# Attention states kept by strips of two heads and read in tiles of 32 rows by 64 columns; the inner gate taken out of PSUM in one copy

## The chip, the cores and the metric

The kernel runs on one core of a Trainium2 chip. The metric is the device time of one execution in microseconds; a shown time is the median over runs. The engines are named as in the profile: PE (TensorE, the matrix engine; PEld is its weight load), DVE (VectorE), ACT (ScalarE), POOL (GpSimd) and SP (SyncE, which here only issues DMAs). PE reads SBUF and writes PSUM, which has eight banks of 128 partitions by 2 KB (512 numbers of f32).

## The reference, cut to what matters

x has 8 rows (batches) of 512 tokens by 512 features. Per row:

```
xn = layernorm(x)
# attention block (16 heads, key width 16, value width 32)
a  = rmsnorm(xn) * ln1
q, k, v, g = a@Wq, a@Wk * scale, a@Wv, a@Wg + bg
gk = log_sigmoid(a @ Wkg1 @ Wkg2 + bkg2) / 16        # Wkg1 is 512 x 16: the "inner gate"
S_t = S_(t-1) * exp(gk_t) + k_t v_t ;  o_t = q_t . S_t   # a scan over tokens, per head
o  = silu(g) * normalized(o) per head
x2 = xn + o @ Wo
s  = x2 + (silu(rmsnorm(x2)@W1) * (rmsnorm(x2)@W3)) @ W2
# gate block: softmax over 8 experts of low rank
out = x + s * silu(sum_e alpha_e * U_e (V_e xn))
```

Products that need full precision are done as three products of high and low parts.

## The kernel before, in words

There are three stages, each over the 8 rows: `phase_f` (layernorm and the gate block), `phase_a` (attention) and `phase_m` (the hidden layer and the output). Each engine has its own instruction stream; semaphores order them. The loops are software pipelined: while the body of a row runs, the parts of the next row are woven in by `ahead(...)`. The body and the parts of `phase_a` are what the change touches.

The scan over tokens is done in NC = 4 chunks c of 128 tokens. Heads and key features lie on partitions: GR = 2 groups g of 8 heads by 16 features, a strip of 32 partitions being two heads. For each chunk PE does, in this order in `body` (L1356 to L1412):

- `weights(i, c)` (L1267, products at L1282): the weights inside the chunk, 64 products per chunk in tiles of 32 rows by 32 columns, into four banks, one for each strip of rows. DVE multiplies them by the causal mask (L1022) into `a_sb`.
- for c < 3: the decayed keys turned (`kt`, L1366); ACT copies them to SBUF (L1203).
- a part of the next row: k0 and k1 at c = 0, u (the inner gate, L1318 and L1320) at c = 1, q0 at c = 2, q1 at c = 3.
- `variance` of the chunk before (L1303), from ACT's squares (L1216).
- for c > 0 the state read (L1390): `state` times the decayed queries, four products of 128 rows by 128 columns ("quads" of four heads) by 128 tokens, into the bank `mix`. The state is kept block-diagonal, 128 by 256 per group, mostly zeros.
- for c < 3 `state_products` (L1351), from which DVE makes the next state: spread over the head mask (L1031) and, for c > 0, decayed and added (L1043).
- the sixteen products of weights and values (L1399), each 32 columns wide, four column strips abreast, into `mix`. ACT squares `mix` (L1216) and copies it (L1219), which frees it.

After the four chunks come, for the next row, z (the key gates, L1329), v0, then the variance of chunk 3, then v1 to v3 and the output gates g0 to g3, and for this row o0 to o3 (all through L160 to L162, 12 products each). ACT's order behind its last copy of `mix` is z (L1140 to L1145), v0, the deviation of chunk 3 (L1231, L1233), `exponentials` (L1156 to L1172), the SiLU of g0 to g3 (L1181). In `exponentials` v1 is copied behind the four exponentials of L1156, v2 and v3 behind those of L1160 and L1162. DVE's `sum_gates` (L945, L950, the scans L954, the three differences L961) feeds them; `gated` (L1063 to L1070) of chunk 3 comes behind, then the weighting of keys and queries (L971 to L994).

PSUM banks are handed out by `Regions`: results take the regions in the order of a list, round robin, and a product waits (`free`) until the result before it in its region has been taken. `dense` has three banks, `mix` one, the weights four. So before, v1's bank was last z1's, g0's was v1's, and g3's was g0's:

```
L845 order = [(None, ["kt0"]), ("k0", ["k0"]), ("k1", ["k1"]), (None, ["ds0", "kt1"]), ("u", ["u"]),
L846          (None, ["var0", "ds1", "kt2"]), ("q0", ["q0"]), (None, ["var1", "ds2"]),
L847          ("q1", ["q1"]), (None, ["var2", "ms"]), ("z", zs), ("v0", values[:1]),
L848          (None, ["var3"]), ("v1", values[1:]), ("g", gates),
```

POOL prepares the attention weights at the start of the span (`prepare_attention_weights`), later it multiplies the loaded xn of the row after by a row factor (`scale`, L1101) and adds squares (L1107). SP issues the loads; the one that POOL's `scale` waits for comes behind a wait for the last `mix` product of a body (L897), a store and a load. In the body of the last row the places of the next row's parts hold first work of `phase_m` (class `Front`).

Of the kernel before, what the change touches and what calls it, by code (L numbers as in the profile page):

```python
# [5 lines left out]
F32 = mybir.dt.float32  # L6
# [50 lines left out]
class Regions:  # L57
# [3 lines left out]
    def __init__(self, counts, name, regions, order, early=()):  # L61
        self.counts, self.name, self.regions = counts, name, regions
        self.where, used = {}, [0] * len(regions)
        for n, result in enumerate(order):
            r = n % len(regions)
            used[r] += 1
            self.where[result] = (r, used[r], 1 if early and result not in early else 0)
# [170 lines left out]
def attention_weights(nc, ctx, KT, D, KD, RANK):  # L238
# [7 lines left out]
    w["wkg1"] = sb("wkg1", [P, KT, 32 + RANK], F32R)  # L246
# [10 lines left out]
def prepare_attention_weights(nc, ctx, pool, w, Wq, Wk, Wkg1, Wkg2, bkg2, Wv, Wg, bg, Wo, ln1_w):  # L257
# [12 lines left out]
    step(pool.memset(w["wkg1"].bitcast(F32), 0.0))  # L270
    RANK, KD = Wkg2.shape
    small = w["stage"][0:RANK, 1, 0:KD]
# [8 lines left out]
    for n, (name, src, kt) in enumerate(jobs):  # L281
# [14 lines left out]
        if name == "wkg1":  # L296
            hi, lo = (w[name][:, kt, at:at + cols] for at in (0, 32))
# [4 lines left out]
    pool.dma_start(small, Wkg2).then_inc(s_small, 16)  # L302
    for dst, src in ((w["bkg2"], bkg2), (w["bg"], bg), (w["ln1"], ln1_w)):
        pool.dma_start(dst, src.rearrange("(m p) -> p m", p=P), allow_slow_non_contiguous=True).then_inc(s_small, 16)
    pool.wait_ge(s_small, 64)
    for at in (0, 32, 96):
        step(pool.tensor_copy(w["wkg2"][at:at + RANK, :], small))
    step(pool.tensor_tensor(w["wkg2"][64:64 + RANK, :], small, w["wkg2"][0:RANK, :].bitcast(F32), ALU.subtract))
# [466 lines left out]
def phase_a(nc, outer, consts, f, shared, w, xn_d, r1_d, xmid_d):  # L775
# [12 lines left out]
    with ctx:  # L788
# [7 lines left out]
        RANK = wkg1.shape[2] - 32  # L796
# [23 lines left out]
        state = [sb(f"state{n}", [P, GR, HG * VH]) for n in range(2)]  # L820
# [7 lines left out]
        psum = [ctx.enter_context(nc.psum_tensor(f"a_ps{b}", [P, 512], F32))[:] for b in range(4)]  # L828
# [3 lines left out]
        for name, per in (("xa_in", 32), ("x2", KT), ("x2sum", KT - 1), ("r2", 1), ("r2_out", 16), ("xn_in", 16), ("xa", KT), ("xahi", KT), ("xalo", KT), ("uhi", 3),  # L832
# [4 lines left out]
                          ("state", GR * (NC - 2)), ("first", NC - 1), ("weighing", NC),  # L837
# [7 lines left out]
        order = [(None, ["kt0"]), ("k0", ["k0"]), ("k1", ["k1"]), (None, ["ds0", "kt1"]), ("u", ["u"]),  # L845
                 (None, ["var0", "ds1", "kt2"]), ("q0", ["q0"]), (None, ["var1", "ds2"]),  # L846
                 ("q1", ["q1"]), (None, ["var2", "ms"]), ("z", zs), ("v0", values[:1]),  # L847
                 (None, ["var3"]), ("v1", values[1:]), ("g", gates),  # L848
                 (None, outs), ("body", [])]
        early = {part: results for part, results in order if part}  # L850
        late = {order[n + 1][0]: results for n, (part, results) in enumerate(order) if not part}
# [1137 lines left out]
```

## Time and profile before

| | |
|---|---|
| median of 3 runs | 1628.15 us (1624.19 to 1628.93) |
| the profiled execution | 1622.4 us, span 1620.7 us |
| PE, PEld | busy 98%, 79% |
| DVE, ACT, POOL | busy 52%, 35%, 10% |
| granted TensorE clock, mean | 0.998 of full |
| attention stage | about 342 to 887 us of the span |
| POOL, busy tenths by slice of 40.5 us, the first nine | 4 7 7 0 0 0 0 1 0 |

The busy shares say which engine sets the pace; the order of time says where one engine waits for another. A matmul of f32 stands as two records in the trace, so "x8" at L1390 are four products; the record's duration includes the modelled tail, and the distance from one start to the next is what it costs.

### The profile page before, as it was taken

The numbers are of one execution on the slowest core, as the hardware profiler recorded it, in microseconds if no ns is written. First come the engines' busy times: TensorE is split into PE (matmuls) and PEld (weight loads), VectorE is DVE, ScalarE is ACT, GpSimd is POOL, SyncE is SP. The second block draws the span as 40 slices with busy tenths as digits, with TensorE's granted clock in tenths as the row PEclk, the third lists the DMA queues.
The fourth block names the chain that finished last, engine by engine and source line by source line (L and its number), as shares of the span: only waits on it lengthen the run. The fifth ranks groups of instructions, "written<-read, shape, count | busy, mean of one in ns | idle before, by whom it ended". The sixth has DMA issues, their size and how long they took to land.

```text
span 1620.7 us, 30581 instructions
## 1 busy us (share of the span) xinstructions
PE 1593.2 (98%) x12274; PEld 1277.6 (79%) x12274; DVE 847.3 (52%) x1311; ACT 567.2 (35%) x982; POOL 167.2 (10%) x190
## 2 busy tenths in 40 slices
PE   7999999999999999999999999999999999999998
PEld 5777888777777777777777788888888888888886
DVE  5565455367797887978876451331415142241413
ACT  4333343366564645636564411111111111111111
POOL 4770000100220102101020000000000000000000
PEclk9999999999999999999999999999999999999999
DMA  7563332101020210202213423030301203030200
GB/s 175 151 135 78 83 95 69 59 27 52 9 84 0 84 53 32 84 0 84 84 54 118 144 101 127 0 136 0 136 0 49 87 0 136 0 136 0 91 14 26
DMA packets 50700, 113.16 MB, mean 70 GB/s; under 512 B 13321, under 2 KB 24665, under 8 KB 42466
## 3 DMA queue, kind: packets, MB, share of 16 engines
q1 hardware_dynamic: 47906, 99.95, 19.5%
q10 hardware_dynamic: 1152, 8.39, 1.3%
q0 software_dynamic: 1600, 4.25, 0.9%
q8 instruction: 28, 0.46, 0.1%
q14 instruction: 14, 0.11, 0.0%
HBM read 78.98 MB, written 33.59 MB: 69 GB/s over the span
## 4 chain that ended last, share of the span: by engine, by line
PE 94%; DVE 2%; ACT 1%; issue 1%; DMA 1%; PEld 0%; SPq 0%; ACTq 0%; DVEq 0%; PEldq 0%
PE m_ps L1529 10%; PE m_ps L1531 10%; PE m_ps L1530 10%; PE a_ps L160 7%; PE a_ps L162 7%; PE a_ps L161 7%; PE f_ps L160 5%; PE f_ps L162 5%; PE f_ps L161 5%; PE m_ps L1543 5%; PE m_ps L1544 5%; PE m_ps L1545 5%; PE a_att L1282 3%; PE a_ps L1399 2%; PE a_ps L1303 2%; PE a_ps L1390 1%
## 5 line engine op out<-in xcount | busy, mean ns | idle before, releaser
L1529 PE MATMUL m_ps<-m_xshi,m_w 128*128 128x512 f32 x680 | 268.1, 394 | 1.4 <-DVE m_w L1520 1.4
L1766 DVE TENSOR_TENSOR m_h<-m_ps,m_silu 128x512 f32<-128x512 f32 x85 | 58.7, 690 | 402.4 <-PE m_ps L1531 402.4
L1531 PE MATMUL m_ps<-m_xshi,m_w 128*128 128x512 f32 x680 | 266.5, 392 | 0.0
L1530 PE MATMUL m_ps<-m_xslo,m_w 128*128 128x512 f32 x680 | 266.4, 392 | 0.0
L1830 ACT ACTIVATE m_silu<-m_ps 128x512 f32<-128x512 f32 x85 | 50.8, 597 | 334.3 <-PE m_ps L1531 334.3
L1529 PEld LDWEIGHTS m_ps<-m_xshi,m_w 128*128 128x128 f32 x680 | 127.7, 188 | 30.0 <-issue 2.1
L1531 PEld LDWEIGHTS m_ps<-m_xshi,m_w 128*128 128x128 f32 x680 | 127.6, 188 | 28.7
L1530 PEld LDWEIGHTS m_ps<-m_xslo,m_w 128*128 128x128 f32 x680 | 127.7, 188 | 28.1 <-issue 0.2
L1101 POOL TENSOR_TENSOR row<-row,a_r 128x512 f32<-128x512 f32 x32 | 50.7, 1615 | 331.6 <-DMA a_r<-scratch_r 331.6
L1022 DVE TENSOR_TENSOR a_a<-a_att,causal 128x1024 f32<-128x1024 f32 x64 | 75.2, 1216 | 11.8 <-PE a_att L1282 11.8
L1839 ACT ACTIVATE m_h0hi<-m_h 128x512 fp32r<-128x512 f32 x46 | 29.1, 632 | 135.7 <-DVE m_h L1766 135.7
L1543 PE MATMUL m_ps<-m_h0hi,m_w 128*128 128x512 f32 x192 | 75.3, 392 | 0.0
L1544 PE MATMUL m_ps<-m_h0lo,m_w 128*128 128x512 f32 x192 | 75.3, 392 | 0.0
L1545 PE MATMUL m_ps<-m_h0hi,m_w 128*128 128x512 f32 x192 | 75.3, 392 | 0.0
L1839 ACT ACTIVATE m_h1hi<-m_h 128x512 fp32r<-128x512 f32 x39 | 24.7, 632 | 115.6 <-DVE m_h L1766 115.6
L1107 POOL TENSOR_TENSOR a_cum<-a_cum 128x512 f32<-128x512 f32 x24 | 30.7, 1281 | 321.3 <-ACT a_cum L1190 321.3
L1543 PE MATMUL m_ps<-m_h1hi,m_w 128*128 128x512 f32 x160 | 62.6, 391 | 0.0
L1544 PE MATMUL m_ps<-m_h1lo,m_w 128*128 128x512 f32 x160 | 62.6, 391 | 0.0
L1545 PE MATMUL m_ps<-m_h1hi,m_w 128*128 128x512 f32 x160 | 62.6, 391 | 0.0
L160 PE MATMUL f_ps<-f_xnhi,f_w1hi 128*128 128x512 f32 x128 | 52.1, 407 | 2.5 <-DVE f_xnlo L476 1.2
L160 PE MATMUL a_ps<-a_wvhi,a_xahi 128*128 128x512 f32 x128 | 53.1, 415 | 0.0
L160 PE MATMUL a_ps<-a_xahi,a_wghi 128*128 128x512 f32 x128 | 50.8, 397 | 0.9 <-ACT a_v_tok L1149 0.6
(306 smaller groups left out, 3487.9 us busy)
## 6 DMA issues: line engine op xcount, KB each, us to landing
row<-scratch_xn SPq DMA_DIRECT2D x16, 1024.0 KB, 4.9
row<-scratch_xmid SPq DMA_DIRECT2D x16, 1024.0 KB, 7.3
m_xt<-in_L_attn_W SPq DMA_DIRECT2D x33, 256.0 KB, 3.2
f_xt<-in_L_attn_x SPq DMA_DIRECT2D x32, 256.0 KB, 8.1
scratch_xn<-row SPq DMA_DIRECT2D x8, 1024.0 KB, 9.0
scratch_gate<-row ACTq DMA_DIRECT2D x8, 1024.0 KB, 3.9
scratch_xmid<-row SPq DMA_DIRECT2D x8, 1024.0 KB, 3.9
row<-scratch_gate SPq DMA_DIRECT2D x8, 1024.0 KB, 10.5
```

Source lines behind the costliest of these rows:

```text
L160: pe.matmul(out, lh, rh, start=first and n == 0, stop=False)
L161: pe.matmul(out, lh, rl, start=False, stop=False)
L162: ins = pe.matmul(out, ll, rh, start=False, stop=last and n == end)
L1022: dve.tensor_tensor(a_sb[n].rearrange("p s g o t -> p (s g o) t"), ps, bcast(causal, 1, 4 * GR), ALU.mult).then_inc(att.taken_sem(f"{c}_{n ...
L1529: pe.matmul(ps, wh, xh, start=k == 0, stop=False)
L1530: pe.matmul(ps, wh, xl, start=False, stop=False)
L1531: ins = pe.matmul(ps, wl, xh, start=False, stop=k == LAST)
L1543: pe.matmul(ps, lh, rh, start=j == 0, stop=False)
L1544: pe.matmul(ps, lh, rl, start=False, stop=False)
L1545: ins = pe.matmul(ps, ll, rh, start=False, stop=j == FT - 1)
L1766: dve.tensor_tensor(h[n], dense.region(f"b{j}"), silu[n], ALU.mult).then_inc(dense.taken_sem(f"b{j}"), 1)
L1839: act.activation(h_hl[n][0], h[n], ACT.Copy).then_inc(count.sem("hhi"), 1)
```

## The change

The state is kept as 128 by 64 per group: a strip of 32 partitions holds its own two heads. The state read takes each strip of 32 rows with its 64 columns, eight products per chunk in place of four. The output of a chunk lies in halves of two banks, EVEN and ODD, for even and odd quads. The turned keys get the other half of ODD. `dense` has two banks of its own and, outside the chunks, ODD as a third; which result takes which is written out in `places`. PE turns the keys of chunks 1 and 2 behind the next row's part, and waits for ACT's copy of them before the state read. z moves behind v0 and the last variance on PE, and behind them and the deviation on ACT. The weights of the inner gate are laid out in four copies (three high, one low) so that one copy on ACT takes all 64 rows out and DVE subtracts one part. POOL prepares these weights.

```diff
@@ attention_weights, prepare_attention_weights
-    w["wkg1"] = sb("wkg1", [P, KT, 32 + RANK], F32R)
+    w["wkg1"] = sb("wkg1", [P, KT, 4 * RANK], F32R)
...
+            copies = [w[name][:, kt, n * RANK:(n + 1) * RANK] for n in range(4)]
+            for copy in copies[1:3]:
+                step(pool.tensor_copy(copy, s))
+            hi, lo = copies[0], copies[3]
@@ phase_a, banks
-        psum = [ctx.enter_context(nc.psum_tensor(f"a_ps{b}", [P, 512], F32))[:] for b in range(4)]
+        psum = [ctx.enter_context(nc.psum_tensor(f"a_ps{b}", [P, 512], F32))[:] for b in range(2)]
+        ps_mix = ctx.enter_context(nc.psum_tensor("a_mix", [P, 2, 512], F32))[:]
...
+        order = [("k0", ["k0"]), ("k1", ["k1"]), (None, ["ds0"]), ("u", ["u"]), (None, ["var0", "ds1"]),
+                 ("q0", ["q0"]), (None, ["var1", "ds2"]), ("q1", ["q1"]), (None, ["var2", "ms"]),
+                 ("v0", values[:1]), (None, ["var3"]), ("z", zs), ("v1", values[1:]), ("g", gates),
+                 (None, outs), ("body", [])]
+        places = {result: n for n, results in enumerate((
+            ["k0", "ds0", "var0", "q0", "ds2", "var2", "v0", "z1", "v3", "g2", "o1"],
+            ["k1", "u", "ds1", "var1", "q1", "ms", "var3", "v1", "g0", "g3", "o2"],
+            ["z0", "v2", "g1", "o0", "o3"])) for result in results}
...
+        dense = Regions(count, "dense", psum + [ps_mix[:, ODD]], ..., places)
+        turned = Regions(count, "kt", [ps_mix[:, ODD, GR * P:]], list(range(NC - 1)))
+        mix = Regions(count, "mix", [ps_mix[:, :, 0:QD // 2 * P]], list(range(NC)))
@@ vector: inner_gate
-                dve.tensor_copy(u[0:RANK], ps).then_inc(count.sem("uhi"), 1)
-                dve.tensor_copy(u[64:64 + RANK], ps).then_inc(count.sem("uhi"), 1)
-                dve.tensor_copy(u[96:96 + RANK], at.region("u")[32:32 + RANK]).then_inc(count.sem("uhi"), 1)
                 dve.wait_ge(*count.at("uhi", i))
-                dve.tensor_tensor(u[32:32 + RANK], ps, u[0:RANK].bitcast(F32), ALU.subtract)...
+                dve.tensor_tensor(u[low], at.region("u")[low], u[low].bitcast(F32), ALU.subtract)...
@@ vector: the next state
-                        for g in range(GR):
-                            ins = dve.tensor_tensor(new[:, g, :]..., bcast(ds[:, g], 1, HG // 2), bcast(hmask...), ALU.mult)
+                        dve.tensor_tensor(new.rearrange("p g (o v) -> p g o v", v=VH), ds,
+                                          bcast(bcast(parity, 1, GR), 3, VH), ALU.mult)...
@@ scalar
+            def inner_gate(i, at=dense):
+                act.wait_ge(*at.ready("u", i))
+                act.activation(u[0:4 * RANK], at.region("u")[0:4 * RANK], ACT.Copy).then_inc(count.sem("uhi"), 1)
...
-                    for part in (("k0", "k1"), ("c1",), ("q0",), ("q1",))[c]:
+                    for part in (("k0", "k1"), ("u",), ("q0",), ("q1",))[c]:
                         ahead(part)
+                    if 0 < c < NC - 1:
+                        keys(i, c)
...
-                ahead("z")
                 ahead("v0")
                 inverse_deviation(i, NC - 1)
+                ahead("z")
                 ahead("exponentials")
@@ tensor: body
+                    for part in (("k0", "k1"), ("u",), ("q0",), ("q1",))[c]:
+                        ahead(part)
+                    if 0 < c < NC - 1:
+                        pe.wait_ge(*mix.taken(c - 1, i))
+                        turned_keys(i, c)
                     if c > 0:
                         variance(i, c - 1)
...
+                    if 0 < c < NC - 1:
+                        pe.wait_ge(*turned.taken(c, i))
...
-                        for quad in range(QD):
-                            g, first_head = quad * HQ // HG, quad * HQ % HG
-                            pe.matmul(ps[:, quad, :], state[c % 2][:, g, first_head * VH:(first_head + HQ) * VH],
-                                      qhat[:, gcs[g], :], start=quad == 0, stop=True, skip_group_check=True)
+                        for g in range(GR):
+                            for strip in range(4):
+                                rows, at = slice(H32 * strip, H32 * (strip + 1)), H64 * (strip % 2)
+                                pe.matmul(ps[2 * g + strip // 2][at:at + H64], state[c % 2][rows, g, :],
+                                          qhat[rows, gcs[g], :], start=g == 0, stop=True, skip_group_check=True,
+                                          tile_position=(H32 * strip, at))
...
-                ahead("z")
                 ahead("v0")
                 variance(i, NC - 1)
+                pe.wait_ge(*mix.taken(NC - 1, i))
+                ahead("z")
                 ahead("v1")
                 ahead("g")
```

The `Front` class takes v0 in place of v1 for one of its products, in the same order of work.

## Rows read from the trace of the kernel before

**Rows 1.** The page: busy time, share of the span and instructions of each engine.
```profile
PE 1593.2 (98%) x12274; PEld 1277.6 (79%) x12274; DVE 847.3 (52%) x1311; ACT 567.2 (35%) x982; POOL 167.2 (10%) x190
```

**Rows 2.** Busy time by stretch: stretch, length, busy us of each engine, clock.
```profile
434.60:501.05 66.45, 66.45 (x939) 52.30 (x943) 53.73 (x72) 37.17 (x66) 10.05 (x7) 1.00 0.13 51
```

**Rows 3.** PE's waits over the span: total us, times, longest.
```profile
PE a_ps L160 <- ACT a_v_tok L1149: 0.6, 2, 0.5
...
PE a_ps L160 <- ACT row L1181: 0.3, 1, 0.3
```

**Rows 4.** PE in order of time, z to g3: start, length, line, records.
```profile
466.39 0.73 PE L1329 MATMUL a_ps<-a_u,a_wkg 128*128 128x512 f32 x2
466.95 0.39 PE L160 MATMUL a_ps<-a_wvhi,a_xahi 128*128 128x512 f32 x1
...
478.81 0.39 PE L160 MATMUL a_ps<-a_xahi,a_wghi 128*128 128x512 f32 x1
...
487.20 0.40 PE L160 MATMUL a_ps<-a_xahi,a_wghi 128*128 128x512 f32 x1
```

**Rows 5.** ACT in order of time, |z| to the first SiLU; idle before in brackets.
```profile
467.50 1.27 ACT L1140 ACTIVATE a_soft<-a_ps,a_bkg 128x512 f32<-128x512 f32 x2
...
475.52 2.29 ACT L1156 ACTIVATE a_lv<-a_lv 128x512 f32<-128x512 f32 x4 [2.67 <-DVE a_lv L961]
477.72 0.58 ACT L1149 ACTIVATE a_v_tok<-a_ps 128x512 f32<-128x512 f32 x1
...
480.24 1.06 ACT L1149 ACTIVATE a_v_tok<-a_ps 128x512 f32<-128x512 f32 x2
...
486.26 1.84 ACT L1181 ACTIVATE row<-a_ps,a_bg 128x512 f32<-128x512 f32 x3
```

**Rows 6.** PE in order of time around chunk 1 and chunk 2.
```profile
447.19 1.02 PE L1303 MATMUL a_ps<-a_sq,avg 128*128 128x512 f32 x2
448.05 1.05 PE L1390 MATMUL a_ps<-a_neg,a_state 128*128 128x128 f32 x8
449.03 0.43 PE L1351 MATMUL a_ps<-a_v_tok,a_fold 128*32 128x64 f32 x16
449.28 1.06 PE L1399 MATMUL a_ps<-a_a,a_v_tok 128*32 128x128 f32 x32
450.27 0.34 PE L1282 MATMUL a_att<-a_qx,a_lv 32*32 32x128 f32 x12
...
451.89 0.44 PE L1366 MATMUL a_ps<-ident,a_soft 128*128 128x128 f32 x2
452.08 0.48 PE L160 MATMUL a_ps<-a_xahi,a_wqhi 128*128 128x512 f32 x1
```

**Rows 7.** DVE in order of time: the first of three inner gate casts.
```profile
447.42 0.67 DVE L931 CAST a_u<-a_ps 16x512 fp32r<-16x512 f32 x1
```

**Rows 8.** ACT in order of time: the deviation of chunk 0, the copy of mix.
```profile
448.25 0.69 ACT L1231 ACTIVATE a_rn<-a_ps,eps 128x512 f32<-128x512 f32 x1 [1.80 <-PE a_ps L1303]
...
452.85 0.60 ACT L1219 ACTIVATE a_oc<-a_ps 128x512 f32<-128x512 f32 x1 [1.85 <-DVE a_rn L1063]
```

**Rows 9.** POOL in order of time: its scaling in the first two looped rows.
```profile
406.82 7.87 POOL L1101 TENSOR_TENSOR row<-row,a_r 128x512 f32<-128x512 f32 x4 [17.28 <-DMA a_r<-scratch_r]
...
478.88 6.21 POOL L1101 TENSOR_TENSOR row<-row,a_r 128x512 f32<-128x512 f32 x4 [21.25 <-DMA a_r<-scratch_r]
```

**Rows 10.** DVE in order of time: the differences L961 in both rows.
```profile
406.14 3.47 DVE L961 TENSOR_TENSOR a_lv<-a_cum 128x1024 f32<-128x1024 f32 x2
409.53 2.31 DVE L961 TENSOR_TENSOR a_dq<-a_cum 128x1024 f32<-128x1024 f32 x1
...
474.26 2.36 DVE L961 TENSOR_TENSOR a_lv<-a_cum 128x1024 f32<-128x1024 f32 x2
```

**Rows 11.** Busy time by stretch at the span's end; PE first, the clock after POOL.
```profile
1610.10:1613.00 2.90, 0.00 (x0) 0.00 (x0) 2.79 (x6) 0.00 (x0) 0.00 (x0) 1.00 0.00 0
...
1614.00:1616.00 2.00, 1.95 (x10) 1.55 (x8) 0.58 (x1) 0.00 (x0) 0.00 (x0) 0.50 0.00 0
```

More of the change, by code:

```diff
@@ L57, with __init__ @@
 class Regions:
-    def __init__(self, counts, name, regions, order, early=()):
+    def __init__(self, counts, name, regions, order, early=(), places=None):
         self.counts, self.name, self.regions = counts, name, regions
@@ L269, in prepare_attention_weights @@
     step(pool.memset(w["wkg2"].bitcast(F32), 0.0))
[L270 removed]
     RANK, KD = Wkg2.shape
[L272 removed]
+    small = w["stage"][0:4 * RANK, 1, 0:KD]
     sources = {"wkg1": Wkg1, "wk": Wk, "wq": Wq, "wv": Wv, "wg": Wg, "wo": Wo}
@@ L819, in phase_a @@
         kt_sb = flat(w["fold"]).rearrange("p (g t) -> p g t", g=GR)
-        state = [sb(f"state{n}", [P, GR, HG * VH]) for n in range(2)]
+        state = [sb(f"state{n}", [P, GR, 2 * VH]) for n in range(2)]
         sq, oc, rn = sb("sq", [P, QD, P]), sb("oc", [P, QD, P]), sb("rn", [P, QD, P])
@@ L1196, in deviation, with keys, by_quads @@
                 act.activation(added[0:1], added[0:1], ACT.Exp, scale=-0.5).then_inc(count.sem("r2"), 1)
+            def keys(i, c):
+                act.wait_ge(*turned.ready(c, i))
+                act.activation(flat(kt_sb), turned.region(c), ACT.Copy).then_inc(turned.taken_sem(c), 1)
+            def by_quads(ap):
+                return ap.rearrange("p (g b) t -> p g b t", b=2)
             def body(i, ahead):
@@ L1354, in state_products, with turned_keys @@
                 ins.then_inc(dense.ready_sem(f"ds{c}"), 1)
+            def turned_keys(i, c):
+                pe.wait_ge(*turned.free(c, i))
+                ps = turned.region(c)
+                for g in range(GR):
+                    ins = pe.transpose(ps[:, g * P:(g + 1) * P], khat[:, g * NC + c, :], ident)
+                ins.then_inc(turned.ready_sem(c), 1)
             def body(i, ahead):
@@ L1379, in body @@
                     pe.wait_ge(*mix.free(c, i))
-                    ps = mix.region(c).rearrange("p (q t) -> p q t", t=P)
+                    ps = [mix.region(c)[:, (EVEN, ODD)[quad % 2], quad // 2 * P:(quad // 2 + 1) * P] for quad in range(QD)]
+                    if 0 < c < NC - 1:
+                        pe.wait_ge(*turned.taken(c, i))
                     if c > 0:
@@ L1433, in tensor @@
             f.tensor(pe, first_row)
-            for part in ("v0", "v1", "g"):
+            parts["v0"](0)
+            pass_over(pe, dense, ["z1"], 0)
+            for m in range(KT):
+                pe.wait_ge(*f.dense.taken(f"u{m}", NB - 1))
+            for part in ("v1", "g"):
                 parts[part](0)
```

107 lines of the change are left out of this document (46 added, 61 removed).

## The prediction

> **What bounds the kernel now.** I read the page's busy times first, then the engines by stage, then PE's waits, then the order of time around the changed places. PE is busy for 98% of the span [rows 1] and for every one of the 66.45 us of an attention row in the middle of that stage [rows 2]; in that row DVE has 53.7 us of work and ACT 37.2. So work taken off PE there comes off the time, work taken off DVE or ACT buys nothing by itself, and any new wait of PE is paid whole. PE's waits in the attention stage are few, and they point at the tight place: for ACT's copy of values (L1149) and for ACT's SiLU of the output gate (L1181), 0.9 us in all [rows 3]. Both are waits of output-gate products (g0, g1 and g3) for a PSUM bank. So I followed the chain that frees these banks: gate products z on PE, absolute value, exponential and logarithm on ACT (L1140 to L1145), sums on DVE (L945 to L961), exponentials on ACT (L1156), and only then ACT's copy of v1 (L1149), behind it v2, v3 and, 8.5 us after the copy of v1, the first SiLU.
>
> In the row of 434.6 to 501.05 PE starts z0 at 466.39 and v0 at 466.95 [rows 4]. ACT starts |z| at 467.50, copies v1 in 477.72 to 478.30, v2 at 480.24, and SiLUs g0 in 486.26 to 486.95 [rows 5]. PE starts g0 at 478.81 and g3 at 487.20 [rows 4]. So the chain has 0.51 us to spare at g0 and 0.25 us at g3.
>
> **The change, part by part.**
> *State read (c = 1 to 3).* Now four products of 128 rows by 128 columns: L1390 starts at 448.05 and L1351 at 449.03, 0.98 us [rows 6]. After: eight products in tiles of 32 rows by 64 columns. L1399 runs sixteen products of 128 moving columns in four column strips in 0.99 us up to the next line's start [rows 6], so a set of four abreast takes at most 0.25 us. If four row strips run abreast too, two sets take 0.50 us, and I add 0.12 us for a second change of tile shape (L1399's four sets of 0.22, as one of L1390's four, leave about that before the 32x32 tiles): 0.62, a gain of 0.36. Bounds: two abreast 0.98 + 0.1, a loss of 0.1; none abreast eight times 0.22 + 0.1 = 1.9, a loss of 0.9. Gains beyond 0.5 would need more than four abreast, which four strips exclude. I take the four, since the 64 products of L1282, which lie in four row strips, take 1.62 us (450.27 to 451.89 [rows 6]), 0.025 each, which no stream of one after the other gives.
>
> The Trainium skill (TensorEngine Tiling, Restrictions and Gotchas) says that different row tiles cannot access the same PSUM bank at once. Strips 0 and 1 share a bank here, 2 and 3 the other, so by that rule it would be two abreast and the loss of 0.1; in this trace L1282 gives every row strip a bank of its own, so no row decides it. It is a rival below.
>
> *Keys turned later (c = 1, 2).* The transposes (0.19 us, 451.89 to 452.08 [rows 6]) move behind u or q0 and behind the mix bank's release, and PE must wait for the keys' copy before the state read. Let U be the end of u (447.19). Transposes and variance (0.86) bring PE to U + 1.05. ACT begins the new u copy at U + 0.23 (DVE's cast did [rows 7]) and the keys' copy 0.5 later; at half the columns of a copy of 0.60 [rows 8] I give it 0.4: U + 1.13, so PE waits 0.1. The mix bank is free earlier: its copy for c = 1 ends at 453.45 [rows 8], and PE wants it behind q0, twelve products of 0.23 from 452.08, at 454.9. The bank of ds1 needs DVE's one subtraction: U + 0.23 + 0.60 + 0.04 + 0.68 = U + 1.55, and PE comes at U + 1.15 + 0.62. Queued on ACT behind the u copy are keys and the deviation, none late. So per body 0.36 + 2 x 0.26 = 0.88 gained, over eight bodies 7.0 us.
>
> *Inner gate in one copy.* Matmul count and moving columns stay (64 and 48 weight columns for 48 and 16), PE nothing. DVE loses three casts (2.1 us a row [rows 7]) and most of the state arithmetic. Both lie beside PE: nothing; at worst DVE's later start would be hidden by the same spare. The longer weight preparation on POOL (eight small copies, three DMAs) is part of its work in the span's first three of forty slices, in the table above; the attention stage comes in the ninth: nothing.
>
> *z behind v0 and the last variance, on PE and ACT.* This is the part that costs. z0 now lies in the bank of the mix, so z goes behind v0 and var3 (0.86 [rows 6]). Between 466.95 and 478.81 lie var3 and 48 value products, 0.229 each; v0 is twelve of them, 2.75 us [rows 4]. In the same row, with v0 at 466.39: var3 at 469.14, z0 at 470.00. ACT is moved too: its logarithm of var3 starts 1.06 after that product (447.19 to 448.25 [rows 6, 8]), so 470.20, lasts 0.69, its exponential 0.63, and |z0| starts at 471.44 in place of 467.50: 3.94 late. v1's bank is now var3's, read till 470.89: PE waits 0.35 there. The chain has no other slack: ACT idles 2.67 us ahead of L1156 for DVE [rows 5], and DVE runs without a gap from the first logarithm's end. DVE's L961 so starts at 474.26 + 3.94 = 478.20.
>
> Here a second thing joins. POOL's scaling of the next x (L1101) starts at 478.88 [rows 9], released by loads that hang on the last mix product, which does not move. In the first looped row it started at 406.82, and there L961's first two and its third took 3.47 and 2.31 us where the undisturbed pair took 2.36 [rows 9, 10]: 2.3 us each beside POOL for 1.17 alone. After the change every row is like that: first L961 to 479.84, second to 482.1, third to 484.4. ACT: exponentials (1.15 the pair) to 483.35, v1 copied 483.25 to 483.85, so g0 starts at 483.90 where PE is ready at 479.2, a wait of 4.7. Then L1160 at 484.45 (waits for the third), v2 at 486.51, 6.27 later than before, and SiLU of g0 from 492.53 to 493.2. g1 waits 0.45 more (v2's bank), g3 0.5 more (g0's). g3 starts 6.27 - 0.25 = 6.0 us late, and so all behind it. Without POOL it would be 3.94 - 0.25 = 3.7.
>
> That is late next and nothing gives it back: the outputs o0 to o3 find DVE free (its weighting ends about 498, o0 at 499), the next body's waits move along. Seven rows are prepared this way (the eighth body has only the next stage's work in these places). The first of them already had POOL and 0.92 us of waits [rows 3]; its L961 would start about 410.8 and its SiLU come about 5 late. Sum: 6 x 6.0 + 5 = 41 lost, 7.0 gained, 34 slower. On the profiled execution's 1622.4 us (span 1620.7) that is 1656.4; the median of the runs lies 5.75 above it, so 1662.
>
> **Rivals.**
> 1. *Two strips abreast* (the shared bank): 24 reads lose 0.1 in place of gaining 0.36, and two a body wait 0.1, so 3 lost for 7 gained: 1672. For: no row shows two row strips in one bank. Against: the column strips of L1399 do share one and run abreast. 20%.
> 2. *POOL does not slow DVE, or starts elsewhere*: 7 x 3.7 - 7 = 19 slower, 1647. For: POOL's start is a DMA's end. Against: [rows 9, 10]. 12%.
> 3. *The clock falls.* After PE's only long gap late in the span (nothing in 1610.1 to 1613.0) the granted clock is 0.50, 1.2 GHz, in 1614 to 1616 [rows 11]. A wait of 4.7 us in every row could do that. g0 at half rate is 2.8 longer; g1 and g3 wait 0.95 anyway, so 1.85 at most is exposed, 13 us over seven rows: up to 1675. Some of it is likely; as a case of its own (over 6 us) 15%.
> The Trainium skill (TensorE: Matmul & The Clock Gate, What's actually happening) says that an idle engine is throttled to 1.2 GHz and activity releases it; [rows 11] agree as to the fall.
> 4. *Faster.* One mechanism: the late z is absorbed before g0, so that only the state read counts: 7 gained, 1621. It decides if the chain from |z| to the copy of v1 has over 3.9 us of slack. For it: DVE is 3 to 4 us a row lighter. Against: that work lies ahead of the chain, and the spare is 0.51 and 0.25 [rows 4, 5]. 7%. That the strips do not run abreast at all: 24 x (0.9 + 0.36) more, 1692, 2%.
>
> **How the numbers follow.** My forecast (four abreast, POOL beside DVE, no more than 6 us from the clock) has 41%: 1662, own range 1656 to 1670. With rivals 1 to 3 on either side the range is 1644 to 1678, leaving out the faster case and the serial strips. A change of 0.3% (4.9 us) is what a measurement can tell. Slower 0.90: all but rival 4 and what lies between; same 0.03, where several of my terms fail at once; faster 0.07.
>
> **What would show it.** In the trace after: PE idle about 4.7 us ahead of the first g product, released by L1149's counterpart, and shorter ones ahead of g1, g3 and v1; |z| about 5 us behind z's old place in the row; L961 near 2.3 us in every row; a PE distance of 0.6 from the state read to the state product; a row of 66.4 + 6.0 - 0.9 = 71.5 us. Wrong if g0 has no wait, if the rows are shorter than 66.4, or if the time from the start of the state read to the next line is near 1.1.

## The result and the profile after

| | before | after |
|---|---|---|
| median | 1628.32 us (1624.19 to 1628.93, 4 runs) | 1676.76 us (1674.34 to 1679.72, 4 runs) |
| ratio | | 1.0314, 95% interval 1.0297 to 1.0332 |
| span of the profiled execution; of a second one | 1620.7; 1622.4 | 1676.9; 1673.6 |

The change makes the kernel 3.1% slower. 1662 (1644 to 1678) was forecast: the direction was right, 15 us of the loss were missing between the medians (20 between the profiled executions, which the parts below are taken from), and by its ratio, 1.0314, the result lies just outside the range, whose upper end is 1.0306 of the 1628.15 it was worked out from.

Words used below: a *body* is one pass over a row's four chunks. There are eight, in three groups: the first pass of the loop (the *first body*), its six later passes (the *looped rows*), and the *last body*, which is written out behind the loop. A wait *marked issue* is time in which PE was idle and waited for nothing that the profile shows. A *narrow* read has tiles of 32 by 64, a *wide* one of 128 by 128.

The page after: busy time, then the chain that ended last. PE's share fell from 98% to 96% of a longer span [rows 1]; DVE's part of the chain is 5% (2% before).
```profile
PE 1608.0 (96%) x12466; PEld 1272.8 (76%) x12466; DVE 821.6 (49%) x1263; ACT 575.0 (34%) x990; POOL 178.1 (11%) x199
...
PE 88%; DVE 5%; issue 3%; ACT 2%; DMA 1%; PEld 0%; SPq 0%; DVEq 0%; ACTq 0%; PEldq 0%
```
PE's waits after (total us, times, longest). The first line answers to L1149's 0.6 us in [rows 3]: it is the wait of g0 in all seven prepared rows.
```profile
PE a_ps L161 <- ACT a_v_tok L1158: 30.4, 7, 7.0
...
PE a_att L1303 <- issue: 6.1, 5, 2.0
...
PE a_ps L161 <- ACT a_rn L1252: 2.2, 7, 0.3
PE m_ps L1566 <- DVE m_w L1557: 2.2, 1, 2.2
...
PE a_ps L161 <- DVE a_xalo L938: 1.5, 1, 1.5
PE a_ps L161 <- PEq L146: 1.2, 1, 1.2
```
Where the time went, by stretch: stretch, length, busy us of PE, PEld, DVE, ACT, POOL, granted clock. First before, cut at its starts of the value products of the first row, the first body, the second, the last, and the place behind its last o product:
```profile
342.33:364.62 22.29, 22.29 (x97) 17.80 (x95) 11.78 (x15) 15.21 (x27) 0.00 (x0) 1.00 0.12 49
364.62:434.62 70.00, 67.47 (x932) 52.04 (x931) 53.41 (x71) 41.73 (x72) 11.71 (x7) 1.00 0.09 35
434.62:501.00 66.38, 66.38 (x932) 52.25 (x931) 53.73 (x72) 37.17 (x66) 10.05 (x7) 1.00 0.13 51
501.00:833.00 332.00, 332.00 (x4652) 261.25 (x4651) 268.66 (x360) 188.25 (x333) 50.28 (x35) 1.00 0.14 55
833.00:885.10 52.10, 50.72 (x862) 39.84 (x861) 39.75 (x60) 26.67 (x46) 3.86 (x3) 1.00 0.25 83
```
Then after, cut at the same places:
```profile
343.46:367.21 23.75, 22.56 (x97) 17.72 (x95) 11.87 (x15) 15.21 (x27) 0.00 (x0) 1.00 0.11 46
367.21:450.51 83.30, 71.53 (x955) 53.70 (x955) 49.51 (x65) 42.38 (x73) 9.35 (x7) 0.92 0.08 30
450.51:522.25 71.74, 67.52 (x955) 51.25 (x955) 49.95 (x66) 38.21 (x67) 11.87 (x7) 0.98 0.12 48
522.25:882.34 360.09, 338.98 (x4772) 257.18 (x4771) 249.82 (x330) 193.42 (x338) 58.80 (x35) 0.97 0.13 50
882.34:936.76 54.42, 50.60 (x885) 37.99 (x885) 37.92 (x57) 27.00 (x46) 3.86 (x3) 1.00 0.24 80
```
Each kernel has a second profile (e12 of after, e13 of before). The loss is the difference of the means over the two, 53.7 us between the spans; between the medians it is 48.4:

| part | before | after | loss | forecast |
|---|---|---|---|---|
| up to the first value products | 342.3, 343.2 | 343.5, 342.1 | 0 | 0 |
| values and gates of the first row | 22.3, 22.3 | 23.75, 23.7 | 1.4 | 0 |
| first body (the loop's first pass) | 70.0, 70.0 | 83.3, 80.7 | 12.0 | 4.1 |
| six bodies | 398.4, 398.4 | 431.8, 431.4 | 33.2 | 30.7 |
| last body and all behind it | 787.7, 788.6 | 794.6, 795.6 | 7.0 | -0.9 |

Five of the six looped rows of after take 71.7 us in the first profile and the last takes 73.25, because the granted clock is 0.50 for longer in it (856.6 to 863.4).

The first looped row of after (450.51 to 522.25) in order of time (start, length; idle before in brackets), PE first, as in [rows 4, 6]. The state read takes 0.59 us from its start to the next line, 0.98 before; |z| waits for z0 and z0 for v0 and the variance:
```profile
479.85 0.67 PE L1420 MATMUL a_mix<-a_neg,a_state 32*64 32x128 f32 x16
480.44 1.08 PE L1430 MATMUL a_mix<-a_a,a_v_tok 128*32 128x128 f32 x32
481.45 0.51 PE L161 MATMUL a_ps<-a_wvhi,a_xahi 128*128 128x512 f32 x1
...
484.33 1.02 PE L1324 MATMUL a_ps<-a_sq,avg 128*128 128x512 f32 x2
484.79 0.79 PE L1350 MATMUL a_mix<-a_u,a_wkg 128*128 128x512 f32 x1
...
486.13 0.50 PE L161 MATMUL a_ps<-a_wvhi,a_xahi 128*128 128x512 f32 x1 [0.32 <-ACT a_rn L1252]
...
498.55 0.79 PE L161 MATMUL a_ps<-a_xahi,a_wghi 128*128 128x512 f32 x1 [3.90 <-ACT a_v_tok L1158]
```
ACT in that row, as [rows 5]: |z0| 5.20 us behind the next products' start (481.45), 1.11 before; then the idle for L972, the copy of v1, the first SiLU.
```profile
486.65 0.67 ACT L1149 ACTIVATE a_soft<-a_mix,a_bkg 128x512 f32<-128x512 f32 x1
...
494.66 1.15 ACT L1165 ACTIVATE a_lv<-a_lv 128x512 f32<-128x512 f32 x2 [4.39 <-DVE a_lv L972]
...
497.92 0.58 ACT L1158 ACTIVATE a_v_tok<-a_ps 128x512 f32<-128x512 f32 x1
...
507.15 0.69 ACT L1190 ACTIVATE row<-a_ps,a_bg 128x512 f32<-128x512 f32 x1
```
DVE's differences L972 in it and, in the first body, its scans L965 (before: four scans 1.37 us), both beside POOL's scaling:
```profile
415.13 4.53 DVE L965 TENSOR_TENSOR_SCAN a_cum<-ones,a_neg 128x128 f32<-128x128 f32 x4
419.59 1.69 DVE L961 TENSOR_TENSOR a_neg<-a_neg,a_soft 128x512 f32<-128x512 f32 x1
...
493.40 3.43 DVE L972 TENSOR_TENSOR a_lv<-a_cum 128x1024 f32<-128x1024 f32 x2
496.75 2.29 DVE L972 TENSOR_TENSOR a_dq<-a_cum 128x1024 f32<-128x1024 f32 x1
```
POOL's scaling in the two bodies:
```profile
415.22 5.51 POOL L1106 TENSOR_TENSOR row<-row,a_r 128x512 f32<-128x512 f32 x4 [20.49 <-DMA a_r<-scratch_r]
...
493.85 8.03 POOL L1106 TENSOR_TENSOR row<-row,a_r 128x512 f32<-128x512 f32 x4 [20.50 <-DMA a_r<-scratch_r]
```
The Trainium skill (SBUF — State Buffer, SBUF: two separate sides) says that DVE instructions with two SBUF inputs and GpSimd instructions that read SBUF shut each other out of a shared port for whole instructions. The trace agrees: a difference of L972 doubles from 1.2 to 2.3 us, and takes 1.23 again where POOL's work is cut (e4).

### The profile page after: what moved, and what is told of

Same layout as the page of the kernel before. It is cut to its first block, busy times and chain, and to the rows that moved or that the text cites. A ratio compares the mean times of both kernels' runs of the same rounds, so it can differ in the third digit from the quotient of the medians.

```text
span 1676.9 us, 30976 instructions
## 1 busy us (share of the span) xinstructions
PE 1608.0 (96%) x12466; PEld 1272.8 (76%) x12466; DVE 821.6 (49%) x1263; ACT 575.0 (34%) x990; POOL 178.1 (11%) x199
## 3 DMA queue, kind: packets, MB, share of 16 engines
q10 hardware_dynamic: 1152, 8.39, 1.2%
## 4 chain that ended last, share of the span: by engine, by line
PE 88%; DVE 5%; issue 3%; ACT 2%; DMA 1%; PEld 0%; SPq 0%; DVEq 0%; ACTq 0%; PEldq 0%
PE m_ps L1566 9%; PE m_ps L1568 9%; PE m_ps L1567 9%; PE f_ps L161 5%; PE a_ps L161 5%; PE f_ps L163 5%; PE f_ps L162 5%; PE m_ps L1580 5%; PE m_ps L1582 5%; PE m_ps L1581 5%; PE a_ps L163 5%; PE a_ps L162 5%; PE a_att L1303 3%; PE a_mix L1430 2%; PE a_ps L1324 2%
## 5 line engine op out<-in xcount | busy, mean ns | idle before, releaser
L1106 POOL TENSOR_TENSOR row<-row,a_r 128x512 f32<-128x512 f32 x32 | 58.6, 1859 | 322.9 <-DMA a_r<-scratch_r 322.9
L161 PE MATMUL a_ps<-a_xahi,a_wghi 128*128 128x512 f32 x96 | 43.4, 452 | 30.4 <-ACT a_v_tok L1158 30.4
L1303 PE MATMUL a_att<-a_qxd,a_dk 32*32 32x64 f32 x2048 | 49.5, 225 | 3.3 <-issue 3.3
```

The costliest lines, as they stand in the source:

```text
L161: pe.matmul(out, lh, rh, start=first and n == 0, stop=False)
L1303: return pe.matmul(ps[s:s + H32, strip % 2, g, :, at:at + q.shape[2]], keys[rows, g * NC + c, s:s + H32], q[rows], start=True, stop=True, ...
```

## The experiments

The ratios are to the runs of before that were made with each experiment, and so do not follow from the medians shown.

**The parts one by one: e1, e2, e3, e8.** e1 is before with z moved only; e2 is after with z first again; e3 is after with the wide read; e8 is before with the new inner gate.
```diff
# e1, in before, PE (the same on ACT); regions as in after
-                ahead("z")
                 ahead("v0")
                 variance(i, NC - 1)
+                ahead("z")
# e2, in after: z0, z1, v0 in regions 0, 1, ODD
+                ahead("z")
+                pe.wait_ge(*mix.taken(NC - 1, i))
                 ahead("v0")
                 variance(i, NC - 1)
-                pe.wait_ge(*mix.taken(NC - 1, i))
-                ahead("z")
# e3, in after
-  pe.matmul(ps[2 * g + strip // 2][at:at + H64], state[c % 2][rows, g, :], qhat[rows, gcs[g], :], ...)  # 8 a read
+  pe.matmul(ps[quad], state[c % 2][:, g, first_head * VH:...], qhat[:, gcs[g], :], ...)                 # 4 a read
```


> The kernel before with one edit: z behind v0 and the variance of chunk 3, on PE and on ACT, with the regions that the change gives them; the state read, the banks of mix and the inner gate stay as before. Theory (the place of z is what costs): the whole loss and none of the gain, so per looped row the measured +5.3 us of the change and the 0.9 us that its state read gives back, 6.2 us; with the first row and the last body as they were measured (+13 and +8), 1628 + 6 x 6.2 + 13 + 8 = 1686 us, and g0 waits about 4 us for the v1 copy in each looped row. Rival (the cost sits in the shared bank of mix and the inner gate's new copy on ACT): near 1628 us, and g0 waits as before. Second rival (instruction fetch or the clock, and not the late z, made the first row and the last body dear): rows +6.2 but the rest as before, 1665 us.

> The changed kernel with z put back ahead of v0 on PE and ACT: z0 and z1 take regions 0 and 1, and v0 takes the bank that mix shares, so v0 waits for ACT's last copy of mix instead of z. Theory: the loss of the change goes and its gain of 7.0 us (0.36 per state read, less the key wait) stays; v0 waits about 0.7 us per row (ACT is done 1.11 us after the products' end in the rows of before, the two z products cover about 0.45), 7 rows, 5 us: 1628.3 - 7.0 + 5 = 1626 us, between 1621 and 1631. Rival (the late z is not the cause, the loss lies in the two banks or in ACT's copy of the inner gate): over 1650 us. If the first row and the last body keep their part of the loss, +10 to +20 on 1626.

> The changed kernel with the state kept block-diagonal again and read in four products of 128 by 128 instead of eight of 32 by 64; z, banks and inner gate as changed. Theory (the narrow read gives 0.36 us a read, 21 to 24 reads, and lies on the path): 1676.8 + 0.36 x 21 = 1684 us, and a read takes 0.95 us where the change shows 0.59. Rival (the gain of the read is swallowed by the wait of g0, since both end at the same copy): within 2 us of 1677. Second rival (the extra products cost instruction time elsewhere): below 1675, and the waits marked issue go.

> The kernel before with the inner gate's part of the change alone (64 rows of products, one copy by ACT, one difference by DVE, the weights laid out for it). Theory (it costs nothing: it lies beside the products of q and the variance): within 1 us of before, a ratio of 0.999 to 1.001. Rival (the 4 us by which the quads read of the changed kernel is dearer than the late z alone come from it, by way of ACT's order or POOL's preparation of the weights): +3 to +4 us, a ratio of 1.002.

| | median | ratio | looped row |
|---|---|---|---|
| e1 late z only | 1676.1 | 1.0319 (1.0301 to 1.0336) | 71.6 to 73.9 |
| e2 z first | 1633.9 | 1.0057 (1.0040 to 1.0074) | 66.4 to 66.5 |
| e3 wide read | 1681.0 | 1.0344 (1.0324 to 1.0364) | 72.9 to 74.0 |
| e8 inner gate only | 1626.75 | 1.0011 (0.9999 to 1.0024) | 66.3 |

The place of z alone makes as large a loss as the whole change (e1: 1.0319 for 1.0314), and taking it back gives all but 0.6% back (e2). e1's first rival, a cost in the shared bank or in the inner gate's copy, falls. Its second, that something else made both ends of the loop dear, falls for the first body and holds for the last, as the stretches show; that is why e1 came out 10 us under what was expected. The three other parts together come to nothing in the span, but not in each stretch. e1 takes 79.8 us in its first body (9.8 over before), 437.2 in the six looped rows (38.8 over) and 788.0 from the last body on (as before). So the other parts win 5.6 us in the looped rows of the change, and lose about 2 in its first body and all of its 7.0 from the last body on. e3 is 5 us above the change (ratios 0.0030 apart). Its looped row has 1.35 us more of reads (1.09, 1.06 and 0.98 from start to next start, for 0.60, 0.59 and 0.59), 9 us over the rows, but its waits marked issue are 2.4 us less (1.7 against the second profile of after) and its end 3.2 us shorter (both below): the narrow read is on the path, and about half of what it wins is lost outside the looped rows. e2's v0 waits as expected:
```profile
PE a_mix L161 <- ACT a_oc L1240: 4.3, 7, 0.6
```

**POOL beside DVE: e4.**
```diff
-  pool.tensor_tensor(xa[:, m, :], xa[:, m, :], by, ALU.mult)
+  pool.tensor_tensor(xa[:, m, 0:16], xa[:, m, 0:16], by[:, 0:16], ALU.mult)
```
This kernel leaves out the row factor for 496 of the 512 tokens.

> The changed kernel with POOL's scale of xn cut to 16 of 512 tokens per instruction (most of the row factor is left out of the computation). Theory (DVE's differences and scans are stretched while POOL works beside them, 3.43 us against 2.3, and 4.53 against 1.37 in the first row): each looped row's g0 wait falls from 3.9 to about 1.6 us, the first row's by 3 or more: 6 x 2.3 + 3.5 = 17 us less, 1659 us. With no wait long enough for a fall of the clock, 1.65 us per row more: 1648 us. Rival (DVE's stretch comes from ACT or from PE reading beside it, not from POOL): L972 stays at 3.4 us and the time within 2 us of 1677.

1662.3 us, 1.0228 (1.0205 to 1.0251). L972's pair is back to 2.38 us, and g0 waits for
```profile
PE a_ps L161 <- ACT a_v_tok L1158: 19.8, 7, 2.8
```
that is 2.8 in every row: POOL costs 1.1 us of this wait in a looped row (not the 2.3 expected, since only the pair ahead of the v1 copy counts, and it starts undisturbed) and 4.2 in the first body, where the scans take 1.37 us again. The looped rows are of two kinds, and the granted clock tells them apart; three of the six are like the first line, three like the second:
```profile
443.91:513.43 69.52, 66.35 (x955) 50.10 (x954) 45.81 (x66) 38.02 (x67) 7.67 (x7) 1.00 0.13 49
513.43:584.28 70.85, 67.70 (x955) 51.41 (x954) 45.80 (x66) 38.13 (x67) 7.67 (x7) 0.98 0.12 48
```
So behind a wait of 2.8 us the clock falls in some rows and not in others, and here a fall costs 1.3 us of the row.

**The clock: e5, e11.** Both put products that nobody reads into PE's wait ahead of g0, so that PE stays busy: 32 of 256 columns (e5), 14 of 512 (e11).
```diff
 def output_gates(i):
+    for _ in range(32):   # e11: 14, into a bank of the weights, 512 columns
+        pe.matmul(ps_mix[:, EVEN, 256:512], wg[0][:, 0, 0:P], xa_hl[0][:, 0, 0:256], start=True, stop=True, ...)
```


> The changed kernel with 32 products of 128 by 128 by 256 ahead of g0, into a half bank that nobody reads, some 3.4 us of work in a wait of 3.9 us. Theory (each looped row loses about 1.5 us to the granted clock of .50 behind the wait for the v1 copy): the wait stays but the first products of g0 come 0.24 us apart instead of 0.43; g takes 11.2 us a row instead of 12.7, 6 x 1.5 = 9 us, and with the first row's fall 10 to 12 us less: 1666 us. Rival (the fall follows from the row's whole share of work and only moves elsewhere, or the products cost what they save): within 2 us of 1677. If they last longer than the wait, each row is later by the difference.

> As e5 with 14 products of 128 by 128 by 512 in place of 32 short ones, about 3.2 us of work in the wait ahead of g0, into a bank of the weights, not in the prologue. Theory (the fall of the clock behind that wait costs 1.5 us a looped row, and e5 lost it again to instruction waits in every row, 2.7 us, because of its many short products): g takes 11.2 us behind the filling, few waits marked issue in the loop, rows of 70.2 us, 1667 us. Rival (any PE instructions added to the loop bring its instruction waits): rows of 73 and more, 1690 us.

In after the clock behind the wait of g0 is at the lower level, 1.2 GHz (one stretch of each row):
```profile
498.20:501.60 3.40, 3.05 (x7) 2.47 (x8) 3.37 (x3) 2.79 (x4) 3.40 (x2) 0.50 0.00 0
```
In e11 it stays at 2.4 GHz through the whole row,
```profile
449.10:520.54 71.44, 70.02 (x969) 52.83 (x968) 50.03 (x66) 38.12 (x67) 11.81 (x7) 1.00 0.12 48
```
and two other waits come out that the slow products had covered:
```profile
493.16 3.43 PE L1362 MATMUL a_att<-a_xahi,a_wghi 128*128 128x512 f32 x14
497.25 0.50 PE L161 MATMUL a_ps<-a_xahi,a_wghi 128*128 128x512 f32 x1 [0.67 <-ACT a_v_tok L1158]
...
500.49 0.50 PE L161 MATMUL a_mix<-a_xahi,a_wghi 128*128 128x512 f32 x1 [0.17 <-ACT a_v_tok L1158]
...
506.63 0.50 PE L161 MATMUL a_ps<-a_xahi,a_wghi 128*128 128x512 f32 x1 [0.28 <-ACT row L1190]
```
g1 starts 3.24 us behind g0 (2.80 at full speed in [rows 4] spacing, twelve of 0.234), g3 9.38 behind it (8.39 there). The row is 71.4 us for 71.7: the fall of the clock costs 1.5 us where it happens and only 0.3 to 0.5 of the row (71.9 in the second profile), because g1's and g3's banks would be late anyway. In e4, where they are not, it cost 1.3. e11: 1671.9 us, 1.0293 (1.0264 to 1.0321), a smaller gain than the 1667 expected. e5 fails in another way: 1700.0 us, 1.0462 (1.0441 to 1.0482). In its first looped row the g0 products run at full speed too, but the loop's code no longer stays loaded; its filling of the first row's wait, before the loop, costs another 3.7 us (27.4 for 23.75). The instruction transfers (queue, packets, MB) in six rows of e5,
```profile
q8 instruction: 54, 0.88, 0.8%
```
and in the same six of e11, as of after and before:
```profile
q8 instruction: 1, 0.02, 0.0%
```
With 987 PE records to a row (e5) nine transfers come in every pass, and PE has waits marked issue in each, 17.5 us over the six; with 969 (e11) it has none. In e5's first looped row they are 2.7 us:
```profile
PE a_ps L1339 <- issue: 1.4, 1, 1.4
PE a_att L1303 <- issue: 1.3, 1, 1.3
```

**A free bank for z: e6.** z1 goes into a bank of the weights, which is free between the last mask and the next row's weights; v0 takes region 1.
```diff
 # in e2
-  dense = Regions(count, "dense", psum + [ps_mix[:, ODD]], ...)
+  dense = Regions(count, "dense", psum + [ps_mix[:, ODD], ps_att[1][:, 1]...], ...)   # fourth: z1
```


> As e2 (z first, narrow read, two banks, new inner gate), but no product waits for ACT's last copy of mix: z1 goes into one of the banks of the weights, whose chunk 3 is masked by then, v0 into region 1, and only the variance of chunk 3 and v3 use the shared bank. Theory: z takes 0.56 us of a row instead of 1.35, 7 x 0.8 = 5.6 us, and the first v0 no longer waits for the stage before, 3 us: 1633.9 - 8.6 = 1625 us, level with before (1624.6) within 0.3%: a row of 65.6 to 65.8 us against 66.39, so 4 to 5 us won in the rows, and given back by the waits marked issue in the first row and the last body, 5 us more than before. Rival (those waits are not the narrow read's and go with another layout): 1620 us, a ratio of 0.997. Rival (the wait moves to the variance of chunk 3 or to v1): over 1630.

1627.2 us, 1.0007 (0.9996 to 1.0018). The looped row is won, as expected:
```profile
436.98:502.59 65.61, 65.61 (x955) 50.37 (x955) 49.72 (x66) 37.76 (x67) 10.02 (x7) 1.00 0.13 52
```
It is 0.8 us a row under before's 66.4, 4.8 over six; the first body is 1.7 longer and the part from the last body on 2.6 to 3.4. So the narrow read is worth 0.8 us a row where nothing waits, 5 us in the looped rows, and these are given back outside them.

**What gives it back: e9, e10, e14, e15, e16.** PE's waits marked issue are 1.4 us in both profiles of before, 6.6 and 5.9 in those of after. e9 is before with each read product cut in two by tokens; e10 is e6 with the wide read in the last body; e14 is before with the keys turned behind the next row's part; e15 is e6 with the keys ahead of it, in banks of their own; e16 is e15 with the old inner gate.
```diff
# e9, in before
+    for t in (slice(0, H64), slice(H64, P)):
-        pe.matmul(ps[:, quad, :], state..., qhat[:, gcs[g], :], start=quad == 0, ...)
+        pe.matmul(ps[:, quad, t], state..., qhat[:, gcs[g], t], start=quad == 0 and t.start == 0, ...)
# e14, in before, PE and ACT, c = 1, 2
-    keys()
     ahead(part)
+    keys()
```


> The kernel before with each of the four products of a state read cut in two by tokens, so that PE has as many instructions per read as in the changed kernel (8 and not 4), and everything else as it was. Theory (it is the number of PE instructions in the unrolled first row and last body that brings the waits marked issue, 6.6 us in the changed kernel against 1.4): those waits rise to 4 to 7 us, beside what the read itself takes more (0.98 now, perhaps 1.2: 21 x 0.2 = 4 us); 1632 us together. Rival (they come with the change's tiles or with where the code lies, not with the count): under 3 us, the looped rows longer only by the reads.

> As e6, but the unrolled first and last rows keep the block-diagonal state and read it in four products of 128 by 128, while the six looped rows read it in eight of 32 by 64. Theory (the narrow products, which follow each other faster, are what makes PE wait for its instructions in the unrolled rows): the waits marked issue fall from e6's 5.8 us to the 1.4 to 4.2 of the kernels with quads there, the reads of the two rows give back 6 x 0.39 = 2.3 us, the looped rows stay at 65.6: 1624.5 to 1627 us, a ratio of 0.998 to 1.001. Rival (the waits are those of the layout with two banks): still 5 us or more, and 1629 us.

> The kernel before with one edit: in chunks 1 and 2 the keys are turned behind the next row's part (u, q0) and not ahead of it, on PE and on ACT, as the change has it; wide read, one bank, old inner gate. Theory (it is this order that brings the waits marked issue: every kernel with it had 4.2 to 6.6 us of them in the first row and the last body, every kernel without it 1.4 to 2.8): 4 us or more of such waits, the looped rows at 66.4 to 66.6, ratio 1.002 to 1.003. Rival (they come from the two banks or the narrow read, or from where the code happens to lie): 1.4 to 2.8 us, ratio 1.000 to 1.001.

> Narrow read, two banks, z first with z1 in a bank of the weights and the new inner gate, as e6, but the keys turned ahead of the next row's part, in banks of their own as before. Theory (order of the keys): rows of 65.5 us, waits marked issue back to 1.4 to 2.8 us, 1622 us where before is 1625.5, ratio 0.998. Rival (the waits stay): 65.5 a row and 5 us of them, ratio 1.000 to 1.001. The reads may start 0.1 to 0.2 us earlier, since the shared bank no longer holds the keys.

> As e15 with the inner gate of before. Theory (the inner gate's part gives 0.1 us a looped row or nothing, as e8 showed): within 0.1% of e15, ratio 0.998 to 0.999. Rival (its copy on ACT and the longer preparation by POOL cost 1 to 2 us before the first row): 1.5 us faster than e15.

| | median | ratio | looped row | issue, first body / last body |
|---|---|---|---|---|
| before, twice | | | 66.4 | 0 / 1.4 |
| e8 | | | 66.3 | 1.2 / 0.6 |
| e1 | | | 71.6 to 73.9 | 1.4 / 0.8 |
| e9 | 1649.1 | 1.0143 (1.0128 to 1.0158) | 68.8 | 1.3 / 1.5 |
| e14 | 1638.6 | 1.0085 (1.0067 to 1.0102) | 67.75 | 1.6 / 2.1 |
| e3 (two banks, wide read) | | | 72.9 to 74.0 | 1.3 / 2.9 |
| e10 | 1629.45 | 1.0027 (1.0016 to 1.0037) | 65.6 | 1.6 / 3.8 |
| e16 | 1636.6 | 1.0067 (1.0054 to 1.0080) | 67.1 | 1.4 / 3.3 |
| e6 | 1627.2 | 1.0007 | 65.6 | 2.0 / 3.2 |
| e15 | 1625.7 | 1.0011 (0.9996 to 1.0026) | 65.6 | 1.7 / 4.2 |
| e2 | | | 66.4 to 66.5 | 1.3 / 4.9 |
| after, twice | | | 71.7, 71.9 | 2.9, 2.2 / 3.7, 3.7 |

In the attention stage of these kernels such waits lie in the loop's first pass and the last body only, where code runs for the first time. (The first body, too, belongs to the loop and is not unrolled, against what I wrote ahead of e9 and e10.) None of my theories explains them alone: not the count of instructions (e9: 2.8 us in the two bodies), not the narrow products (e10, whose last body has none and waits 3.8 us), not the order of the keys (e14 has 3.7, between what the theory and its rival wanted; e15, with the old order, has 5.9). Kernels with `mix` in two banks have 4.2 us or more in the two bodies (e3 the least) and the others 3.7 or less (e14 the most). The two profiles of after differ by 0.7, more than lies between e3 and e14, so this is no clean line either; the cause is open. e9's 17 us above what was expected are mostly its reads, 1.82 us each for 0.98, 2.5 a row (last section).

e14 and e16 brought something else. Their looped rows lose 1.3 and 1.5 us to one wait that neither before nor after has (PE's waits in e14):
```profile
PE a_ps L1355 <- DVE a_u L935: 8.9, 7, 1.3
```
The old inner gate, three casts and a difference on DVE, still holds u's bank when the state product of chunk 1 wants it; with the new one the wait is gone (e15 against e16: 10.9 us between the medians, 1.5 us a row). I had put the new inner gate at nothing, which is true of before's banks (e8) and false of the change's.

**The same code again: e12, e13.**

> The changed kernel, unaltered, for a second profile of the same code. The theory of steps (first row, six rows, last body) wants the same looped rows of 71.7 us and the same 7 us wait in the first row; if the 3.7 us at the very end (11.3 us from the last transposes to the end of the span, against 7.6) is chance, it comes out at 7 to 9 us here, and the waits marked issue show how much they move by themselves.

> The kernel before, unaltered, for a second profile. If the start of the attention stage (342.3 us in the first profile, 343 to 344 in the kernels whose stage before is the same) moves by 1 us, and the waits marked issue (1.4 us) move too, then 1 to 2 us of the difference between two profiles belong to no edit; the looped rows must come out at 66.4.

Of e12 by stretch, first body and second:
```profile
365.86:446.56 80.70, 69.58 (x955) 52.30 (x954) 49.51 (x65) 42.38 (x73) 9.35 (x7) 0.94 0.08 31
446.56:518.46 71.90, 67.70 (x956) 51.47 (x955) 49.95 (x66) 38.22 (x67) 11.76 (x7) 0.98 0.12 47
```
Rows repeat within 0.2 us. The first body does not: 2.6 us less here, with k and q1 at full speed, where the first profile had them at the lower clock, 1.5 us more each; the second has it for longer around g0's wait instead. The end is no chance: from the last transposes to the end of the span it takes 11.3 and 10.9 us, 7.6 and 8.4 in before. After, SP's issues of the four output stores:
```profile
1669.43 4.74 SPq L1766 DMA_DIRECT2D out<-m_xt  x4
```
Before:
```profile
1616.14 2.12 SPq L1729 DMA_DIRECT2D out<-m_xt  x4
```
In the last 12 us of after, two instruction transfers fall between the first store and the end, none in before's:
```profile
q14 instruction: 2, 0.02, 0.5%
```
The other traces bear out that these transfers go with the late stores. Of the seventeen profiles, five (after, e12, e4, e5, e11) have two transfers 5.5 to 5.8 and 3.3 to 3.6 us before the end; in each the second store comes 3.3 us behind the first, and the end takes 10.1 to 11.3 us. The twelve others have none in the last 10 us; there the stores are 0.6 us apart and the end takes 7.0 to 8.4, in e3 too (8.1), which is after with the wide read. No run moved the transfers and nothing else, so that they delay the stores is likely and not shown.

## Why the prediction was off

The step that failed is the carrying over of the looped row's sum to the bodies at both ends of the loop: they were priced at 4.1 and -0.9 us and cost 12.0 and 7.0. The items follow the prediction's terms.

- *What bounds the kernel, and the step that costs*: right. z behind v0 is the loss, by the chain |z|, DVE, exponentials, v1, g0. e1 and e2 show it. In the looped rows e3, e6, e8 and e15 clear the other parts.
- *State read*: 0.59 us for 0.62 forecast, so four strips run abreast (two would need 1.08), though strips 0 and 1 share a bank. Rival 1 is refuted. The rule of the Trainium skill (TensorEngine Tiling (Array Packing), Restrictions and Gotchas) that different row tiles cannot access one PSUM bank at the same time does not hold here, for two row strips that write different partitions of it. Strips that write the same partitions of a bank were not tried. The gain in a looped row is 0.76 (1.17 from the reads, less 0.2 ahead of the reads of chunks 1 and 2 together, and 0.2 ahead of chunk 3's), not 0.88.
- *The looped row*: 71.5 forecast, 71.7 and 71.9 measured. That this is so near is in part luck, since terms cancel (forecasts in brackets). v1 waits 0.32 (0.35). g0 waits 3.9 (4.7): POOL's start falls 0.45 us behind the start of the first difference and stretches the pair by 1.05 (1.5, from 478.20 to 482.1 for 2.36), and PE comes to g0 0.4 later. That is because z1's region is v0's, which was not counted: z1 waits for v0's copy, which ends at 485.13, and z takes 0.4 more. g1 and g3 do not wait (0.95), since g0 at the lower clock is 1.5 longer; e11 takes the fall of the clock away and finds them at 0.44 and 0.55, as forecast.
- *The first body*: this term failed, 12.0 against 4.1. I took "POOL was there already" for "little more to lose", with L961 moved and POOL fixed. But the chain moved so that POOL met the scans, 4.53 us for 1.37, and g0 waits 7.0 us; e4 takes 4.2 of it away. e1, where only z is late, has the same 7.0 us wait and 9.8 of the 12.0. To these come waits marked issue of 2.9 and 2.2 us (none before, 1.4 in e1) and, in one profile of two, 3.1 of the clock. The 410.8 that the prediction gives for L961's start here should by its own 3.94 be 410.1, which changes little.
- *The last body and the end*: this term failed, 7.0 against -0.9. The prediction said only that this body prepares no row, and counted nothing for it but the read's gain; no row I used showed the waits marked issue, and I took unrolled code as free. 2.3 us are these, 3.1 lie behind the last transposes (2.6 of them SP's later stores), and 0.8 and 0.6 are a longer wait for `m_w` (2.2 and 2.05 us for 1.4 and 1.5). In e12 some 1.6 are left, and there the granted clock is 0.50 behind that wait, as it is not in the first profile. e1 has none of the 7.0, so it is not the late z's; what makes the waits longer is open.
- *The first row's values*: 1.4, forecast 0. PE hands z1's region on between v0 and v1 and so waits for ACT's copy of v0 (PEq, PE's own sequencer, 1.2); e1, which has the same order, takes 23.5, and e2 and e6, without it, take 22.4 and 22.3.
- *Rival 3* (the clock) came true as a mechanism: g0's products take 1.5 us more in each looped row. As a price it is 0.3 to 0.5 of most of these rows, against the 1.85 at most that were forecast. The last looped row and the first body of the first profile, and the place behind the `m_w` wait in the second, lose about 1.5 to each further stretch at the lower clock. *Rival 2* is refuted by e4. *Rival 4* is refuted by g0's wait.

## What to carry to other kernels

Before you order a step behind a longer one because of a bank that they share, ask what hangs on it: here two products of 0.56 us feed a chain of 12 us (z0 to the v1 copy) with 0.5 us to spare, and a bank of the weights, idle at that time, carries one of them (e6). Price the copies that empty a bank by who wants the bank next, not by their engine's load (e14, e16). Six looped rows that win 0.8 us each are worth nothing if the loop's first pass and the unrolled last body pay about as much: price those apart. No version tried beats before; e6 and e15 equal it.

## What the runs showed of the hardware that was not expected

- A product of 128 by 128 with 64 moving columns takes as long as one with 128: in e9 eight take 1.82 us, 0.23 each, where four of 128 take 0.98, 0.245 each. What binds them was not tested.
```profile
454.50 1.89 PE L1391 MATMUL a_ps<-a_neg,a_state 128*128 128x64 f32 x16
456.32 0.43 PE L1351 MATMUL a_ps<-a_v_tok,a_fold 128*32 128x64 f32 x16
```
- A loop's code stays loaded up to some size and is transferred anew in every pass beyond it: 1 transfer in six passes with 969 PE records a pass, 54 with 987.
- Short DVE instructions lose the most time beside POOL, because each of them pays: four scans took 4.53 us for 1.37, 0.8 more each, and one long difference 2.29 for 1.22, 1.1 more. In e1 the same four scans take 4.54 us, and in e4, where POOL's work is cut, 1.37.
- Behind waits of 3.9 us ahead of g0 the granted clock fell in every looped row of after, behind waits of 2.8 us in three of six (e4).
